# Cross-attention of a fused Perceiver block: weighted values moved directly behind the scores, output stages moved by one place

## What is computed

```
Q = LN(x) Wq.T + bq ; K = ctx Wk.T + bk ; V = ctx Wv.T + bv      # x (32,32,512), ctx (32,257,512)
scores = Q K.T / sqrt(32)                                        # 16 heads of 32
scores = where(scores <= softplus(raw_thresholds), -1e9, scores)
x = x + (softmax(scores) V) Wo.T + bo
```

```
x = x + retention_layers(LN(x))     # 2 layers, 8 heads of 64, feed-forward of 2048
x = x + experts(LN(x))              # 8 experts, 2 per token, hidden 1024
```

## Time and profile before

| | |
|---|---|
| Median of 3 runs | 1672.0 us (1669.37 to 1674.09) |
| The profiled execution | 1671.4 us, its span 1669.6 us |
| PE busy | 1602.9 us, 96% of the span |
| DVE, ACT, POOL busy | 1007.1, 850.3, 420.8 us |
| Cross-attention with prologue and tail | 0 to about 544 us of the span |

### The profile page before, as it was taken

How to read it: one execution, slowest core, us unless ns; L and a number is a source line. 1 busy time by engine, 2 the same in 40 slices (tenths; PEclk the granted TensorE clock), 3 DMA queues, 4 the chain that set the end, 5 groups by cost and what they waited for, 6 DMA issues and landing times.

```text
span 1669.6 us, 31234 instructions
## 1 busy us (share of the span) xinstructions
PE 1602.9 (96%) x11984; PEld 1342.3 (80%) x11984; DVE 1007.1 (60%) x2002; ACT 850.3 (51%) x1195; POOL 420.8 (25%) x357
## 2 busy tenths in 40 slices
PE   7999999999998799999998999999989999999997
PEld 6888888888887688788877887878877888888886
DVE  4343443443446676644347676644449999999995
ACT  4554444444444333353343333534418888878883
POOL 1333333323332444200005442200021212212111
PEclk9999999999999999999999999999989999999999
DMA  5111111111112200222332002234250553636612
GB/s 199 37 33 36 38 38 29 34 38 38 56 45 72 89 2 1 64 85 87 106 133 77 1 2 64 89 113 144 97 221 19 189 176 127 216 92 242 212 35 70
DMA packets 35839, 143.76 MB, mean 86 GB/s; under 512 B 4977, under 2 KB 5361, under 8 KB 28529
## 3 DMA queue, kind: packets, MB, share of 16 engines
q1 hardware_dynamic: 30592, 130.65, 22.7%
q0 software_dynamic: 5168, 12.06, 3.6%
HBM read 222.39 MB, written 12.85 MB: 141 GB/s over the span
## 4 chain that ended last, share of the span: by engine, by line
PE 59%; DVE 4%; DMA 2%; ACT 1%; issue 1%; SPq 0%; POOL 0%; DVEq 0%; POOLq 0%; ACTq 0%
PE bank L99 36%; PE bank L1623 10%; PE bank L2098 7%; PE bank L1518 2%; PE bank L2104 2%; PE bank L1531 1%; DVE e_w L2025 1%; DMA wraw<-in_wa 1%; PE bank L1607 1%; DMA A<-xh_d,token 1%; DMA out<-acc_d 0%; PE bank L1642 0%; DMA acc_d<-A,token 0%; DVE X L1493 0%; DVE A L1493 0%
## 5 line engine op out<-in xcount | busy, mean ns | idle before, releaser
L2025 DVE TENSOR_TENSOR e_w<-e_raw,e_w 128x2048 fp32r<-128x2048 f32 x134 | 302.4, 2284 | 20.6 <-ACT e_w L1907 20.1
L1907 ACT ACTIVATE e_w<-e_raw 128x2048 fp32r<-128x2048 f32 x134 | 256.7, 1918 | 37.5 <-PE bank L2098 17.7
L99 PE MATMUL bank<-e_w,e_xT 128*128 128x512 f32 x1104 | 272.2, 396 | 0.0
L99 PEld LDWEIGHTS bank<-e_w,e_xT 128*128 128x128 f32 x1104 | 204.7, 189 | 41.5
L99 PE MATMUL bank<-ctx,wk 128*128 128x258 f32 x1536 | 200.2, 287 | 0.0
L99 PE MATMUL bank<-x2T,fw 128*128 128x512 f32 x768 | 189.3, 396 | 5.6 <-DVE fw L1327 5.6
L99 PEld LDWEIGHTS bank<-ctx,wk 128*128 128x128 f32 x1536 | 188.5, 191 | 1.4
L1623 PE MATMUL bank<-fw,hh 128*128 128x512 f32 x768 | 185.1, 390 | 2.6 <-DVE hh L1445 2.6
L99 PEld LDWEIGHTS bank<-x2T,fw 128*128 128x128 f32 x768 | 145.1, 190 | 35.8 <-issue 5.8
L1623 PEld LDWEIGHTS bank<-fw,hh 128*128 128x128 f32 x768 | 143.8, 188 | 33.4 <-issue 2.2
L610 DVE TENSOR_SCALAR_CACHE_REDUCE u<-bank,thr 128x257 f32<-128x257 f32 x128 | 54.5, 483 | 165.7 <-PE bank L805 165.7
(11 more groups left out here) (254 smaller groups left out, 2522.9 us busy)
## 6 DMA issues: line engine op xcount, KB each, us to landing
e_raw<-in_we SPq DMA_DIRECT2D x138, 1024.0 KB, 5.2
fraw<-in_wf SPq DMA_DIRECT2D x64, 512.0 KB, 3.6
ctxraw<-in_ctx SPq DMA_DIRECT2D x32, 514.0 KB, 3.5
wraw<-in_wa SPq DMA_DIRECT2D x20, 512.0 KB, 4.5
X<-in_x SPq DMA_DIRECT2D x4, 512.0 KB, 6.8
acc_d<-X SPq DMA_DIRECT2D x8, 256.0 KB, 5.6
xh_d<-A SPq DMA_DIRECT2D x8, 256.0 KB, 4.1
out<-acc_d SPq DMA_DIRECT2D x4, 512.0 KB, 5.9
```

The source lines that it names most:

```text
L99: last = nc.tensor.matmul(out, lhs(t, a), rhs(t, b), start=start and n == 0, stop=n == len(steps) - 1)
L1907: nc.scalar.activation(w[pos][:, 0, :, :], raw[pos][:, :, :], ACT.Copy).then_inc(m["w_hi"], 1)
L2025: nc.vector.tensor_tensor(w[pos][:, 1, :, :], raw[pos][:, :, :], r(w[pos][:, 0, :, :]), ALU.subtract).then_inc(m["w_lo"], 1)
```

## The change

On PE, the weighted values of element b-2 leave the middle of the K products of element b and come directly behind its scores, ahead of the second half of V. Their waits (probabilities turned, V copied, bank 7 read) stand ahead of the last chunk of V's first half. In the place that they left a wait on `pT_ok` remains, since the third K product writes bank 4. The projection of the group before moves from k = 1 to k = 2 and waits for `oT_ok`; the wait on `x1_sum` moves from k = 2 to k = 3.

On ACT, the copy of V's first half waits for the weighted values of b-2 (they read the buffer that it writes), and `heads_hi` moves from k = 1 to k = 2. On DVE, `heads` and `bias_heads` move behind the threshold and the softmax terms of the same element, `project_lo` from k = 1 to k = 2, and `add_x` from k = 2 to k = 3.

PE's program gets four runs of fill products: 20 at the very start (on a tile that POOL sets to ones), 10 and 7 in the tail, 10 at the end of it. In the prologue the transpositions of x tiles 4 to 7 come after the first, first, second and third query product in place of the first to the fourth, and ACT and DVE follow.

```diff
 PE, prologue
+pe.wait_ge(warm_set, 1)
+spin(nc, bank[7], pT[:, 0, 0, :], 20)
 ...
-for n in range(4):
-    query(n)
-    turn_x(4 + n)
+query(0)
+turn_x(4)
+turn_x(5)
+query(1)
+turn_x(6)
+query(2)
+turn_x(7)
+query(3)
 PE, loop
                                 if dc == 1 and not (first and k < 2):
-                                    if not (first and k == 2):
-                                        pe.wait_ge(oT_ok, b - 2)
-                                    attend((k - 2) % BPT, b - 2, it if k == 2 and not first else None)
+                                    pe.wait_ge(pT_ok, 2 * b - 2)
 ...
                                 if c == DC - 1:
                                     score_waits(b, begin)
+                                    if not (first and k < 2):
+                                        if not (first and k == 2):
+                                            pe.wait_ge(oT_ok, b - 2)
+                                        attend_waits(b - 2, it if k == 3 and not first else None)
 ...
                             score()
+                            if not (first and k < 2):
+                                attend((k - 2) % BPT)
 ...
-                            if k == 1 and not first:
+                            if k == 2 and not first:
+                                pe.wait_ge(oT_ok, b - 1)
                                 project(it - 1)
 PE, tail
                     pe.wait_ge(oT_ok, NB - 2)
-                    attend(BPT - 2, NB - 2, None)
+                    spin(nc, bank[7], ident[:, :], 10)
+                    attend_waits(NB - 2, None)
+                    attend(BPT - 2)
 ...
-                    attend(BPT - 1, NB - 1, None)
+                    attend_waits(NB - 1, None)
+                    attend(BPT - 1)
+                    spin(nc, bank[5], ident[:, :], 7)
                     pe.wait_ge(e["xn_lo"], 1)
 ...
+                    spin(nc, bank[5], ident[:, :], 10)
 ACT
-                                if dc == 3 and k == 1 and not first:
+                                if dc == 0 and k == 2 and not first:
                                     heads_hi(it - 1)
 ...
+                            if not (first and k < 2):
+                                act.wait_ge(pv_ps, b - 1)
                             nc.scalar.activation(v[k % 2][:, 0, :], bank[0][:, :], ACT.Copy).then_inc(v_ok, 1)
 DVE
                             if k == BPT - 1 and not first:
+                                add_x(it - 1)
                                 statistics(it - 1)
                             final = last and k == BPT - 1
                             if k == 2 and not first:
-                                add_x(it - 1)
-                            if not (first and k < 2):
-                                heads((k - 2) % BPT, b - 2)
-                            if k == 1 and not first:
-                                bias_heads(it - 1)
                                 project_lo(it - 1)
 ...
                             softmax_terms(b)
+                            if not (first and k < 2):
+                                heads((k - 2) % BPT, b - 2)
+                            if k == 1 and not first:
+                                bias_heads(it - 1)
 POOL
+nc.gpsimd.memset(pT[:, 0, 0, :], 1.0).then_inc(warm_set, 1)
```

More of the change, by code:

```diff
@@ L91, in spin @@
     for _ in range(n):
-        nc.tensor.matmul(bk[:, 0:P], ident[:, :], ident[:, :], start=True, stop=True)
+        nc.tensor.matmul(bk[:, 0:P], ident, ident, start=True, stop=True)
 def products(nc, out, terms, lhs, rhs, start=True):
@@ L440, in _ @@
                     act.wait_ge(vec_in, 16)
-                    for n in range(4):
[L442 to L446, removed]
+                    query_hi(0)
+                    turned_hi(4)
+                    turned_hi(5)
+                    query_hi(1)
+                    turned_hi(6)
+                    query_hi(2)
+                    turned_hi(7)
+                    act.wait_ge(ctx_in[0], 16)
+                    nc.scalar.activation(ctx[0][:, 0, :, 0:SK], ctxraw[0][:, :, :], ACT.Copy).then_inc(ctx_hi, 1)
+                    query_hi(3)
                     weight_hi(1)
@@ L576, in _ @@
                     statistics_of(range(4, 8))
-                    for n in range(4):
-                        normalise_x(4 + n)
-                        turned_lo(4 + n)
+                    normalise_x(4)
+                    normalise_x(5)
+                    turned_lo(4)
+                    normalise_x(6)
+                    turned_lo(5)
+                    normalise_x(7)
+                    turned_lo(6)
+                    turned_lo(7)
                     weight_lo(1)
@@ L785, in attend @@
                             pe.wait_ge(x1_sum, t_sum)
+                    def attend(k):
                         for c in range(DC):
@@ L1711, in _ @@
                 for t in range(NT // 2, NT):
-                    spin(nc, bank[R_BANK[t]], ident, 7 if t == NT // 2 else 3)
+                    spin(nc, bank[R_BANK[t]], ident[:, :], 7 if t == NT // 2 else 3)
                     router_turn(t)
@@ L2075, in tensor @@
             def tensor(pe):
-                spin(nc, bank[6], ident, 6)
+                spin(nc, bank[6], ident[:, :], 6)
                 pe.wait_ge(q["both_ok"], 1)
@@ L2080, in tensor @@
                 nc.tensor.matmul(bank[4][:, NT * NE:2 * NT * NE], ones, flat, start=True, stop=True).then_inc(q["cnt_ps"], 1)
-                spin(nc, bank[6], ident, 32)
+                spin(nc, bank[6], ident[:, :], 32)
                 pe.wait_ge(q["carried_ok"], 3)
@@ L2143, in body @@
                     down(D0, 0)
-                spin(nc, bank[6], ident, 14)
+                spin(nc, bank[6], ident[:, :], 14)
                 turn_x(0, 0)
-                spin(nc, bank[6], ident, 4)
+                spin(nc, bank[6], ident[:, :], 4)
                 tiles(pe, body)
```

4 lines of the change are left out of this document (2 added, 2 removed).

## The result

The changed kernel takes 1651.7 us (median of 4 runs, 1650.3 to 1656.9) against 1671.5 (4 runs, 1669.4 to 1674.1). The ratio is 0.9892, with a 95% interval from 0.9871 to 0.9913: 14.5 to 21.6 us faster. The profiled execution took 1651.8 us, its span is 1650.0, 19.6 shorter than before.

What follows compares the result with a forecast made beforehand. PE, busy for 96% of the span, was taken as the bound. Gains of 8.0 + 3.0 + 3.2 + 0.5 = 14.7 us off the profiled 1671.4 gave 1656.7 us, range 1651.0 to 1663.5.

Steps and rivals of the forecast that it cites:

- stall: In the loop, PE's wait for add_x, seven times, would be covered and vanish: 8.0 us gained.
- place of the weighted values: In the loop, weighted values directly behind the scores would cost 0.10 us less per element over thirty elements: 3.0 us gained.
- prologue: Before the loop, reordered transpositions hide the last split and start fills may raise the clock: 3.2 us gained.
- tail: After the loop, fills hold the clock through turn, 1.2 us gained, but the last fills delay PE: 0.5 us left.
- everything behind the barrier: Stages after the barrier: no term in the sum; a differing length there would show the prediction wrong.
- the third rival: Whole kernel: clock held through the prologue and 0.14 us gained per element, giving 1653.1 us; chance 9%.
- The bound that had V's load idle 0.41 us behind them: In the loop, worst case for the weighted values' new place: 0.27 us more per element, 8.1 us lost.
- the rival at the scores' pace: In the loop, weighted values behind the scores take 0.69 us more for 30 elements, 20.7 us: 1680.4 us; chance 5%.
- The wait of the projection: In the loop at k = 2, the projection's wait for heads would be covered by 0.15 us and cost nothing.
- The second rival: Clock low again when query products begin: prologue gains 1.5 us, tail -0.4, giving 1659.3 us; chance 18%.
- one of the prediction's own signs of being right: In the prologue, a first query product of about 3 us would show the prediction right.
- one of being wrong: A stage behind the barrier that differs in length would show the prediction wrong.

Runs made afterwards that it cites:

- the first experiment: The kernel before with the projection at k = 2 and add_x at k = 3, weighted values left between the halves of K: 1672.1 us, ratio 1.0014.
- the third experiment: The changed kernel with the old prologue order and none of the four new runs of fill products, the loop change alone: 1651.4 us, ratio 0.9894.
- the fourth experiment: The kernel before with only the new prologue order (1667.4 us, timed once); a second kernel, the kernel before with only the 20 start fill calls (1669.7 us, timed once).

## Why the prediction was right, and where its sizes were off

The five terms, forecast and measured in the two profiled executions: stall 8.0 and 8.6, place of the weighted values 3.0 and 5.4, prologue 3.2 and 3.9, tail 0.5 and 0.3, everything behind the barrier 0 and 1.3. The sum is 14.7 against the span's 19.6, a third more. What was right is the way of the change and its largest term. The time also lies outside the narrower 1654 to 1660 that the forecast gave to its own mechanism (60%), and nearest to the third rival (1653.1, 9%), whose first condition, the high clock through the prologue, was not met: that the number came so near to it is chance.

**The stall: right.** 8.0 us were taken away, 8.6 went. The 0.6 is the restart: PE's stream loses 1.23 us where the wait is listed with 1.16. That the cover comes from the new place was argued, and is shown by the first experiment.

**The price of the place: too small.** 0.10 us per element and 3.0 in all were predicted, 0.18 and 5.4 came. This is the term that was mis-sized most, and it failed at its reference. The unbroken K was read off at element 1, 5.86 us. There K follows V's 512-column products, and its first load starts 0.2 us ahead of its first matmul; in the earlier trace rows K follows the short spread, where load and matmul start together. In the changed kernel's trace K takes 5.86 (54.67 to 60.53) at element 1 again, and 5.74 at element 2. Measured like with like, the weighted values cost 6.64 - 5.74 = 0.90 us between the halves of K, and 0.70 in their new place. The bound that had V's load idle 0.41 us behind them, and the rival at the scores' pace, did not come: 0.67 us of loads for 64 records is their pace from before.

On the rule of the Trainium skill, TensorEngine Tiling (Array Packing), section Tiling Modes, that a change of mode drains the engine: one change less saved 0.18 us, between the cheapest and the dearest idle time. The rule names what is saved; at the mean price of four changes it would have given 6.7 us, nearer to the 5.4 than the sum's 3.0.

**The wait of the projection: right**, with a cover of 0.3 us for the computed 0.15.

**The prologue: near in size, by luck, and wrong in picture.** 3.2 us were predicted, 3.9 measured between these two executions. The order's part is 1.7 to 1.8 us (1.55 predicted). The rest is not shown to be a property of the kernels: K of element 0 started at 46.73, 46.75 and 43.08 us in three executions of the same prologue, and at 42.79, 40.92, 43.97, 41.93 and 42.85 in five of the new one. The eleven executions without fills between them put the 32-column products at 3.8 to 6.9 us. The profile of before happened to be one of the slow ones, and the sum took its pace as given. The second rival, the clock low again at the first query product, is what happened, and cost 1.5 us of that product alone (4.48 against 2.98), but the 32-column products had run fast in part. So one of the prediction's own signs of being right, a first query product of about 3 us, did not appear, and one of being wrong did: the code behind the barrier changed its length.

**The tail: right.** The clock held through `turn` gains 0.96 for a predicted 1.2, and the last run of fills costs 0.62 of it for a predicted 0.7: 0.3 are left for a predicted 0.5.

**What was left out.** Behind the barrier the code is unchanged, and its length was taken as fixed. Over the fourteen profiled spans it ran from 1115.8 to 1125.2 us, and the mean granted clock was 0.987 in the longest and 0.993 in the shortest. The pace of the loop differs between executions too: in nine of the changed loop an element without projection takes 13.92 us in four and 13.89 in five, steadily from the third element to the last, on the same chip too. This scatter is larger than what the fills do, and it is enough for a kernel with the loop's change only not to be told from the full one by time.

## What to carry to other kernels

A wait that repeats once per group and is queued behind unrelated work is worth its idle time and a little more; move the waiting instruction, not only the one that it waits for, and then look which short cover you have uncovered. Take a reference duration from a place with the same neighbours, and compare matmul starts with matmul starts. Fill products did their work here right ahead of the dense work that needs the clock and in idle time; behind the last work ahead of a barrier they only made PE late. Before crediting a stretch with 2 us, look at the same stretch in two more executions.

## What the runs showed of the hardware

- The clock of the first 20 us differs between executions: the same 32 products of 32 columns, behind the same transpositions, took 6.93 us in one and 3.88 in another on the same chip (the first and the third experiment; their programs differ only behind this place). In the third the pace was fast from 12.15 us on, and the granted clock was 0.50 from 15.5 to 18.8.
- Transpositions alone can stand ahead of a rise of the clock: in the third and the fourth experiment PE had run nothing but 16 records of them (from 8.49 and 8.53 us) when the 32-column products began at the fast pace, 0.12 us each. In the kernel before, the same 16 were followed by the slow pace.
- Runs of four fill records (0.69 us) between groups of eight 32-column products (0.98 us) kept the fast pace up to the first query product in three of three executions; without them the clock was low during that product in eleven of eleven.
- The same idle time of 2.81 us ahead of a product was followed by the low clock in one execution (4.58 us for the product) and by the high one in another (2.97).
- Where the array goes from the scores to the weighted values, the next load idles 0.41 us, as it did when full-size products followed the scores; from the weighted values to full-size products it doesn't idle measurably (0.04 us).
